# Cross attention and a two-layer local-attention block on one core: the layers' scores in one stretch, their value products in another, a new order on every engine, and the clamp on GpSimd

## The reference, cut to what matters

```python
h = shift_token(x)                 # second half of the channels one token later
q, k, v = split(h @ wqkv, 3)       # 256 -> 3 x 512, 8 heads of 64
q, k = l2norm(q) * qs, l2norm(k) * ksc
q, k = rotary_xpos(q, k)
o = local_attention(q, k, v)       # windows of 128, each looks at itself and the one before
x = x + o @ wo
h = (h - mu) / sqrt(var + 1e-05) * lg + lb     # of the shifted x
a, g = split(h @ w1 + b1, 2)       # 2 x 682
x = x + (a * gelu(g)) @ w2 + b2
```

## Time and profile before

| | us |
|---|---|
| median of 3 runs | 1418.66 |
| the three runs | 1416.92, 1418.66, 1420.14 |
| profiled execution, first to last instruction (span) | 1416.2 |
| busy in it: TensorE / VectorE / ScalarE / GpSimd | 1385.3 / 1090.6 / 935.8 / 761.9 |
| mean granted TensorE clock | 1.000 |

### The profile page before, as it was taken

How to read it: one execution, slowest core, us unless ns; L and a number is a source line. 1 busy time by engine, 2 the same in 40 slices (tenths; PEclk the granted TensorE clock), 3 DMA queues, 4 the chain that set the end, 5 groups by cost and what they waited for, 6 DMA issues and landing times.

```text
span 1416.2 us, 32735 instructions
## 1 busy us (share of the span) xinstructions
PE 1385.3 (98%) x11563; PEld 1237.8 (87%) x11563; DVE 1090.6 (77%) x3067; ACT 935.8 (66%) x2662; POOL 761.9 (54%) x576
## 2 busy tenths in 40 slices
PE   8999999989999999999999999999999999999998
PEld 7999998778888888888888888888888888888887
DVE  5777776768788788888888878778778888888874
ACT  6877777456666666666666667666666666666662
POOL 1212222556566566666666667666656666666653
PEclk9999999999999999999999999999999999999999
DMA  5223122101100100010001211111111111111001
GB/s 190 90 92 110 48 67 90 47 20 29 30 30 30 30 29 28 28 28 28 28 29 29 71 29 37 33 35 37 37 37 37 36 36 36 36 36 37 29 30 31
DMA packets 50516, 63.41 MB, mean 45 GB/s; under 512 B 8402, under 2 KB 32104, under 8 KB 50408
## 3 DMA queue, kind: packets, MB, share of 16 engines
q1 hardware_dynamic: 50408, 61.99, 14.0%
HBM read 38.17 MB, written 16.78 MB: 39 GB/s over the span
## 4 chain that ended last, share of the span: by engine, by line
PE 65%; DVE 16%; ACT 9%; issue 5%; DMA 2%; POOL 1%; SPq 1%; DVEq 0%; ACTq 0%; POOLq 0%
PE pb L567 30%; PE pb L880 6%; PE pb L894 6%; PE pb L856 5%; PE pb L825 5%; PE pb L840 5%; ACT x_p L1079 4%; PE pb L920 4%; DVE p_t L1596 2%; DVE p_t L1610 2%; ACT x_pt L1085 2%; DVE r_sin L1583 2%; DVE n_sq L1562 2%; DMA x<-x 1%; DVE r_cos L1577 1%
## 5 line engine op out<-in xcount | busy, mean ns | idle before, releaser
L1823 POOL TENSOR_TENSOR n_inv<-n_cl,half_neg 128x16 f32<-128x16 f32 x64 | 211.2, 3299 | 178.2 <-DVE n_cl L1567 174.7
L1222 ACT ACTIVATE p_t<-p_t,s_nm 128x128 f32<-128x128 f32 (+1 forms) x512 | 227.0, 447 | 22.3 <-DVE s_nm L1596 20.9
L567 PE MATMUL pb<-h_hi,w_hi 128*128 128x256 f32 x704 | 207.5, 295 | 1.3 <-DVE h_lo L1558 1.2
L567 PE MATMUL pb<-h_hi,w_lo 128*128 128x256 f32 x704 | 198.7, 282 | 0.0
L567 PE MATMUL pb<-h_lo,w_hi 128*128 128x256 f32 x704 | 198.6, 282 | 0.0
L1828 POOL TENSOR_TENSOR r_cos<-r_cos,r_sin 128x1024 f32<-128x1024 f32 x64 | 154.6, 2415 | 53.8 <-DVE r_sin L1583 53.8
L1213 ACT ACTIVATE pt_t<-pb 128x512 f32<-128x512 f32 x192 | 114.3, 597 | 98.5 <-PE pb L840 97.8
L1178 ACT ACTIVATE qk_sq<-pb 128x512 f32<-128x512 f32 x128 | 72.5, 592 | 142.9 <-PE pb L567 141.5
L567 PE MATMUL pb<-wqkv_hi,xt_hi 128*128 128x512 f32 x384 | 163.9, 427 | 2.6 <-DVE r_sin L1583 2.3
L1859 POOL TENSOR_TENSOR hg_lo<-hg,hg_hi 128x256 fp32r<-128x256 f32 (+1 forms) x192 | 141.9, 760 | 44.5 <-DVE hg_hi L1627 44.5
L1596 DVE CUSTOM_DVE_ANT_0 p_t<-pb,mask_t 128x128 f32<-128x128 f32 (+1 forms) x512 | 151.9, 353 | 17.5 <-PE pb L825 17.3
(11 more groups left out here) (145 smaller groups left out, 3907.5 us busy)
## 6 DMA issues: line engine op xcount, KB each, us to landing
y_state<-x SPq DMA_DIRECT2D x32, 256.0 KB, 2.0
x_cur<-y_state SPq DMA_DIRECT2D x32, 256.0 KB, 2.6
x_res<-y_state SPq DMA_DIRECT2D x32, 256.0 KB, 2.8
x_in<-x SPq DMA_DIRECT2D x16, 256.0 KB, 2.9
x_state<-x SPq DMA_DIRECT2D x16, 256.0 KB, 2.0
x_orig<-x_state SPq DMA_DIRECT2D x16, 256.0 KB, 2.9
out<-x SPq DMA_DIRECT2D x16, 256.0 KB, 2.2
x<-x SPq DMA_DIRECT2D x32, 112.0 KB, 2.3
```

The source lines that it names most:

```text
L567: mm = pe.matmul(dst, s, m, start=(n == 0 and k == 0), stop=(n == len(pairs) - 1 and k == 2))
L1222: e = nc.scalar.activation(pu, pu, ACT.Exp, bias=s_nm[:, j, k:k + 1], scale=-1.0, accum_out=s_sum[:, j, k:k + 1])
L1823: nc.gpsimd.tensor_tensor(n_inv[:, t], n_cl[:, t], half_neg[:], ALU.pow).then_inc(pool_inv, 1)
```

## The change

The arithmetic stays. Changed are the order of the steps on all engines, the bank tables that this needs, one buffer, and the engine of the clamp.

- **Scores.** The six units get six banks, `S_BANK = [0, 7, 3, 4, 5, 6]`. PE issues scores 0, 1 and 2 back to back at the head of the round.
- **Value products.** `weigh` becomes `weigh_late` (units 0, 1, then 2, 3) and `weigh_early` (units 4, 5): 48 matmuls back to back, behind all transposes of the probabilities.
- **Probabilities in place.** `probs_copy` writes the transposed unit back to `p_t`; `pt_t` and ScalarE's waits for its four places are gone.
- **PE's other work.** `turn_h` comes early, behind two feeds. The transposes of q and k are split in two pairs with hidden 5 between. The next item's first projection (k of tile 0) moves from the head of the round to the end of the round before.
- **Clamp.** VectorE's `clamp` goes; GpSimd does it in `inverse_norms`, ahead of the power.
- **VectorE** begins with the statistics and the maxes 0 to 2; `norm_h`, `split_h` and `rotate(a, 0)` come earlier, `second_residual` behind `rotate(a, 0)`, the residual ahead of the last gates. **ScalarE** begins with the exponentials of unit 0; copies of q and k are split by the last gelu. **GpSimd** has the second tile's `add_parts` ahead of its `inverse_norms`.
- **Fillers.** In round 1 the 6, 26 and 11 are gone, 5 stay.
- Loads and stores, matmul counts and shapes are as before.

```diff
-        S_BANK = [3, 4, 3, 4, 3, 4]
-        PT_BANK = [5, 7, 5, 7, 5, 2]
-        QT_BANK = [5, 4, 1, 2]
+        S_BANK = [0, 7, 3, 4, 5, 6]
+        PT_BANK = [5, 7, 5, 7, 5, 7]
+        QT_BANK = [5, 4, 7, 2]
+        QKV_BANK = {(0, 0): 0, (0, 1): 1, (0, 2): 2, (1, 0): 2, (1, 1): 3, (1, 2): 6}
...
+            def weigh_late(a, b, par, half):
+                if half == 0:
+                    pe.wait_ge(act_pt, at(b, UNITS, 2))
+                    pe.wait_ge(act_v, at(b if a is None else a, NT, NT))
...
 PE, a full round
+                    scores(a, b, c, d, 0)
+                    scores(a, b, c, d, 1)
+                    scores(a, b, c, d, 2)
...
+                    turn_h(b, c)
...
+                    weigh_late(a, b, was, 0)
+                    weigh_early(b, was)
+                    weigh_late(a, b, was, 1)
...
+                    turn_qk(a, b, c, 0)
+                    turn_qk(a, b, c, 1)
+                    hidden(a, b, c, 5)
+                    turn_qk(a, b, c, 2)
+                    turn_qk(a, b, c, 3)
+                    project(plus(a, 1), a, c, 0, 1)
...
-                nc.scalar.activation(pt_t[:, u % 4], pb[:, PT_BANK[u]], ACT.Copy).then_inc(act_pt, 1)
+                nc.scalar.activation(p_t[:, u], pb[:, PT_BANK[u]], ACT.Copy).then_inc(act_pt, 1)
...
-            def clamp(a, t):
-                dve.wait_ge(dve_ss, at(a, NT, t + 1))
-                nc.vector.tensor_scalar(n_cl[:, t], n_sq[:, t], NORM_MIN_SQ, None, ALU.max).then_inc(dve_cl, 1)
...
             def inverse_norms(a, t):
-                pool.wait_ge(dve_cl, at(a, NT, t + 1))
+                pool.wait_ge(dve_ss, at(a, NT, t + 1))
+                nc.gpsimd.tensor_scalar(n_cl[:, t], n_sq[:, t], NORM_MIN_SQ, None, ALU.max).then_inc(pool_cl, 1)
+                pool.wait_ge(pool_cl, at(a, NT, t + 1))
                 nc.gpsimd.tensor_tensor(n_inv[:, t], n_cl[:, t], half_neg[:], ALU.pow).then_inc(pool_inv, 1)
```

More of the change, by code:

```diff
@@ new lines, in weigh_early @@
+            def weigh_early(b, par):
+                pe.wait_ge(act_pt, at(b, UNITS, UNITS))
+                for k in range(4):
+                    for u in (4, 5):
+                        h = heads_of(u)[k]
+                        r, col = (h % 2) * DH, (h // 2 % 2) * T
+                        mm = pe.matmul(pb[r:r + DH, 6 + h // 4, col:col + P], v_t[:, par, 0, h * DH:h * DH + DH],
+                                       p_t[:, u, k * P:k * P + P], start=True, stop=True)
+                mm.then_inc(pe_av, 1)
@@ L863, in feed @@
+            def feed(b, c, d, k):
                 if k == 0:
-                    if c is not None:
+                    if b is not None:
+                        pe.wait_ge(dve_max, at(b, UNITS, 2))
+                    elif c is not None:
                         pe.wait_ge(dve_olo, at(c, 2, 2))
@@ L940, in run_l @@
                     return
+                if isinstance(g, int) and g == ITEMS:
+                    for j in range(3):
+                        scores(a, b, c, d, j)
+                    for k in range(5):
+                        feed(b, c, d, k)
+                    turn_p(b, d, 0)
+                    feed(b, c, d, 5)
+                    idle_products(16, 1)
+                    turn_h(b, c)
+                    for u in range(1, 5):
+                        turn_p(b, d, u)
+                    hidden(a, b, c, 0)
+                    turn_p(b, d, 5)
+                    weigh_late(a, b, was, 0)
+                    weigh_early(b, was)
+                    weigh_late(a, b, was, 1)
+                    hidden(a, b, c, 1)
+                    out_product(b, 0)
+                    out_product(b, 1)
+                    for m in range(2, FC):
+                        hidden(a, b, c, m)
+                    return
@@ L962, in run_l @@
-                if d is not None:
-                    feed(c, d, 3)
-                    feed(c, d, 4)
-                if b is not None:
-                    scores(a, b, 2)
-                    turn_p(a, b, d, 0)
-                if a is not None and not is_first(a):
-                    project(a, d, 1, 1)
-                if d is not None:
-                    feed(c, d, 5)
-                if last_attention:
-                    idle_products(16, 1)
+                    feed(b, c, d, 0)
+                    feed(b, c, d, 1)
@@ L981, in run_l @@
-                if is_first(a):
-                    pe.wait_ge(dve_rope, NT)
+                    turn_p(b, d, 0)
+                if a is not None and not is_first(a):
+                    project(a, b, c, 1, 0)
+                    project(a, b, c, 1, 1)
+                if d is not None:
+                    feed(b, c, d, 5)
+                if c is not None:
+                    hidden(a, b, c, 0)
+                if b is not None:
+                    turn_p(b, d, 1)
+                if c is not None:
+                    hidden(a, b, c, 1)
@@ new lines, in run_l @@
+                if a is not None and not is_first(a):
+                    project(a, b, c, 1, 2)
+                if b is not None:
+                    turn_p(b, d, 2)
+                    turn_p(b, d, 3)
+                if c is not None:
+                    hidden(a, b, c, 2)
+                if b is not None:
+                    turn_p(b, d, 4)
+                if c is not None:
+                    hidden(a, b, c, 3)
+                if b is not None:
+                    turn_p(b, d, 5)
@@ L1015, in run_l @@
                     out_product(b, 0)
-                if c is not None and not last_attention:
-                    hidden(a, b, c, 5)
+                    out_product(b, 1)
                 if a is not None:
@@ L1700, in run_l @@
                 if b is not None:
-                    inverse_sums(b, 3)
-                    norm_probs(b, 1)
-                    norm_probs(b, 2)
+                    maxes(b, 3)
+                    inverse_sums(b, 0)
+                    norm_probs(b, 0)
                     maxes(b, 4)
-                    norm_probs(b, 3)
-                if d is not None:
-                    second_residual(d, 1 - par, layer)
-                if b is not None:
-                    inverse_sums(b, 4)
-                if a is not None and not is_first(a):
-                    clamp(a, 0)
-                if b is not None:
-                    norm_probs(b, 4)
+                if fresh:
+                    squares(a, 0)
                 if c is not None:
@@ L1736, in run_l @@
                     gate(c, 0, layer)
+                if has_next(a):
+                    x_lo(plus(a, 1))
+                if is_first(a):
+                    y_normed(SEQS - 1)
+                if c is not None:
+                    gate_hi(c, 0)
+                    gate(c, 1, layer)
                 if b is not None:
```

386 lines of the change are left out of this document (176 added, 210 removed).

## The result

The changed kernel takes **1457.3 us** (median of 4 runs, 1456.47 to 1459.39), beside 1419.4 for the kernel before on the same chip: ratio 1.0272, interval 1.0260 to 1.0285. It is slower where 1379 was forecast, and the range of 1368 to 1402 doesn't hold it. The profiled execution has a span of 1455.0 us, against 1416.2 before and 1376.8 in the sum: 78.2 us are missing.

The account below looks back on a forecast made before the run. PE's list was taken as the bound: 29 rounds x (1.18 - 0.15) = -29.9, with -2, -3.5, -3.0 and -1 making -39.4. Span 1416.2 becomes 1376.8, plus 2.4 about 1379 us; range 1368 to 1402.

Parts of the forecast that it names:

- the sum: All forecast savings added, -39.4 us, taken from the profiled span of 1416.2: a span of 1376.8 us.
- What bounds the kernel: PE's list is the bound: 35.30 us a full round; only a shorter list wins, as 7.9 us is lost above pace.
- the seams: On PE, entering and leaving half-height stretches costs time; merging saves 0.86 us on scores, 0.32 on value products, 1.18 a round.
- Do the others keep up?: Step laying other engines' new lists against PE's 34.1 us round: they fit, with rooms of 0 to 2.6 us.
- three `norm_probs` with reciprocals 2.1: VectorE behind second_residual: 2.1 us for these steps, within 6.2 us in all before hidden 3.
- the room of 1.2 ahead of hidden 3: VectorE needs 6.2 us from the last feed to the second rotation; PE has 7.4 us of work until hidden 3.
- Rival 1: New waits on PE take back 0.6 to 0.9 us of each round's 1.18: 1396, up to 1405 us; chance 0.19.
- Rival 3: Second tile's rotation late behind two GpSimd products, 4.3 us; hidden 3 waits 3.1 a round: 1469 us; chance 0.05.
- the clamp of 16 columns that took 1.60: VectorE's clamp at 672.10 ended with GpSimd's addition at 673.7; its removal was counted as nothing, only room.
- Clamp: Moved to GpSimd, ahead of the power: estimated 0.3 us, bounded by under 0.1 and 3.3.
- Rounds 1 and 2: Round 2 starts some 3.5 us earlier, near 291.5, and round 2 itself gets 3.0 us shorter.
- The clock's fall in round 1: Without fillers PE idles some 3 us at a time; a fall of the granted clock would cost 1 to 2 us.

Follow-up runs that it names:

- experiment 1: Changed kernel plus two GpSimd waits, so norm_qk of tile 0 and add_parts of tile 1 start after VectorE's norm_probs: 1395.61 us, ratio 0.9837 to the kernel before.
- experiment 6: experiment 1 plus three full-height filler matmuls, after scores 0, after scores 1 and inside the value products: 1428.01 us, ratio 1.0056 to the kernel before.
- experiment 7: Kernel before plus one GpSimd wait for reciprocals, delaying the first tile's add_parts to run beside VectorE's norm_probs: 1482.56 us, beside 1419.24 (one run).
- experiment 8: Changed kernel with norm_probs as one tensor_scalar per head, reading one SBUF tile instead of two: 1457.13 us, ratio 1.0261 to the kernel before.
- experiment 9: experiment 5 with the clamp back on VectorE behind squares and GpSimd's clamp removed: 1380.65 us, ratio 0.9736 to the kernel before.
- experiment 11: Changed kernel with inverse_sums and norm_probs 5 ahead of the second tile's rotation, no wait added: 1455.11 us, ratio 1.0260 to the kernel before.
- experiment 5: experiment 1 with gate_hi 1 behind out_lo 1, and next loads and residual among and behind later gates: 1381.23 us, ratio 0.9725 to the kernel before.
- experiment 4: Changed kernel with 24, 24 and 40 filler matmuls in round 1, where PE waits: 1457.66 us, ratio 1.0288 to the kernel before.

## Why the prediction was wrong

- **What bounds the kernel, and the seams: right.** PE was the bound, its list could get shorter without losing a matmul, and a full round with PE always busy is 34.04 us (experiment 1), 1.26 less than before; the sum had 1.18. Putting three breaks back costs 1.35 with their fillers, some 1.02 without (experiment 6), so the seams were put a little too high. By the Trainium skill (TensorEngine Tiling (Array Packing), Key Properties) a change of tiling mode drains the array; the runs agree, at about 0.4 us for going in and out.
- **The step that failed: "Do the others keep up?", the durations of `norm_probs`.** I laid VectorE's new list out with the durations of the earlier trace rows, "three `norm_probs` with reciprocals 2.1", all taken where GpSimd had no product running. The same list says of another place that casts of VectorE stretch beside GpSimd's elementwise work; the effect was known there and put at nothing here. In the new order GpSimd's `norm_qk` of the first tile and `add_parts` of the second fall on them. The three took 1.7 us more, which ate the room of 1.2 ahead of hidden 3 and made it 0.8 late (the rest is other steps a little longer than laid out); `norm_probs` 5 took 2.2 more, where PE had 0.7 to spare, and made `turn_p` 5 another 1.5 late.
- **Rival 1 named the mechanism, and mis-sized it.** It let `norm_probs` 5 wait for `add_parts` and had `turn_p` 5 0.3 us late; the wait measured is 1.5. It let the step come 1.7 late, as if its own 0.7 ran along with the addition; it came 2.2 late, since 0.55 of its work follows the addition's end. And it left PE 1.4 to spare, where PE had 0.7. It missed the first collision altogether. As evidence against it I took the one `norm_probs` beside the power. That row shows the power, and says nothing on a product.
- **Rival 3, slower, had the right direction and a chance of 0.05.** Two products in VectorE's way, hidden 3 late by 3.1 us a round, 1469. There were two, but only the first stood ahead of hidden 3 (0.8 late); the second made `turn_p` 5 late (1.5), and 2.3 and 1457 came. What was held against it, that `second_residual` waits for PE anyway, didn't help: it did wait 1.1 us, but the hold-up came behind it. The row that should have raised its chance was quoted in the prediction: the clamp of 16 columns that took 1.60 and ended with GpSimd's addition. I read it as a small thing that goes away; it was the same hold-up, and in the new order it would act on the steps that PE waits for.
- **The page's rule.** The Trainium skill (GPSIMD Engine Reference, Specifications, the row on SBUF interfaces) says that GpSimd contends with VectorE instructions in a 2-port mode or with two SBUF inputs. For `norm_probs` that agrees. The Trainium skill (SBUF — State Buffer, Who interferes with whom) counts `cast` and `tensor_scalar` among the instructions that can enter a 2-port mode, and has whoever issues first keep the shared pair of ports for the whole instruction, while the other is blocked. The trace agrees for the one-tile forms, the clamp and the casts (experiments 1, 7 to 9 and 11), and for the ends 0.03 to 0.55 us behind the product; it doesn't for GpSimd's power, 3.3 us long, beside which nothing was held up.
- **Clamp: right.** 0.26 for an estimate of 0.3, and no effect on the time.
- **Rounds 1 and 2: wrong, apart from the collision.** Even without it (experiment 5) round 2 begins at 296.35 and the third at 330.08, against 291.5 and 323.7: 6.4 us late. The first score is at 265.7 and not 263.3, which the plan left where it was (2.4, which may be chance: in the eleven profiles of the new order it lies between 262.3 and 267.3); round 1 is 30.6 where 28.2 were planned (2.4), and round 2 33.7 for 32.2 (1.5). The clock's fall in round 1 came, to 0.74 in the changed kernel, and restoring it won nothing (experiment 4).
- **The size, had the collision been seen.** Experiment 5 has a span of 1382.1 against the sum's 1376.8: 6.4 late at the third round, 6.4 gained in the 29 rounds (993.3 in place of 999.7: most are 34.04, where the sum had 34.12 and 0.15 lost), and 5.3 more after the last first score, which wasn't looked into.

## What to carry to other kernels

A duration read from a trace belongs to what the other engine did at that moment. When a change moves steps against each other, list for each moved SBUF step of VectorE which GpSimd instruction will run beside it, and let it begin its own length only at that instruction's end; a tiny step with a long record is the sign to look for. Where GpSimd has room, a wait that starts its long elementwise product after VectorE's due steps, beside VectorE's PSUM reads or reductions, can be worth it: two gave 62 us here.

Matmuls of another height than their neighbours belong together in one stretch: each stretch of 8 to 32 such matmuls cost 0.3 to 0.4 us on PE here. Such a gain is real and small, and exists only while the lists of the other engines fit into PE's.
